# Three instead of four VectorE operations per Newton round of the layer norms of a two-layer decoder

## The reference

```
def _layernorm(x, axis=-1, eps=1e-05):
    m = jnp.mean(x, axis=axis, keepdims=True)
    v = jnp.var(x, axis=axis, keepdims=True)
    return (x - m) / jnp.sqrt(v + eps)

x = _layernorm(x + _L0_attn_ref(x, ...), axis=-1)     # norm 1
x = _layernorm(x + _L0_xattn_ref(x, ctx, ...), axis=-1)   # norm 2
x = _layernorm(x + _L0_ffn_ref(x, ...), axis=-1)      # norm 3
x = _layernorm(x + _L1_attn_ref(x, ...), axis=-1)     # norm 4
x = _layernorm(x + _L1_xattn_ref(x, ctx, ...), axis=-1)   # norm 5
x = _layernorm(x + _L1_ffn_ref(x, ...), axis=-1)      # norm 6
```

## Time and profile before

| | us |
|---|---|
| median of 3 runs | 2399.1 |
| lowest and highest | 2398.3 and 2404.93 |
| the profiled execution | 2404.64 |
| its span, first to last instruction | 2402.8 |

### The profile page before, as it was taken

The page is one execution under the profiler, slowest core; times in us unless marked ns, Lnnn a source line. Parts: engine busy times, 40 slices in busy tenths (PEclk is TensorE's granted clock), DMA queues, the critical chain, the costliest instruction groups (busy, mean ns, idle before and its releaser), DMA issues.

```text
span 2402.8 us, 41468 instructions
## 1 busy us (share of the span) xinstructions
PE 2027.9 (84%) x14592; PEld 1537.6 (64%) x14592; DVE 1495.6 (62%) x4040; ACT 821.1 (34%) x1665; POOL 910.0 (38%) x940
## 2 busy tenths in 40 slices
PE   5687889878998789887899878998789977899797
PEld 3444677655776467673776646865477655777586
DVE  5466466665775657756667657665576655765654
ACT  2112333342333334333343333333333342333342
POOL 2002533442335333353334433344233542335364
PEclk8577899998999789997899879999789988999898
DMA  5001000010000100001000000000000010000000
GB/s 155 3 1 31 3 1 1 1 32 3 3 1 2 34 3 1 1 2 34 3 1 2 21 15 3 2 1 23 13 3 1 1 33 1 3 1 1 11 1 5
DMA packets 25889, 27.75 MB, mean 12 GB/s; under 512 B 16482, under 2 KB 22348, under 8 KB 25188
## 3 DMA queue, kind: packets, MB, share of 16 engines
q1 hardware_dynamic: 25668, 24.88, 3.8%
HBM read 18.83 MB, written 1.05 MB: 8 GB/s over the span
## 4 chain that ended last, share of the span: by engine, by line
PE 53%; DVE 22%; issue 15%; POOL 7%; ACT 2%; DVEq 0%; POOLq 0%; ACTq 0%
PE ps L810 5%; PE ps L839 4%; PE ps L841 4%; PE ps L840 4%; DVE xmax_x L1547 4%; PE ps L858 4%; PE ps L859 4%; POOL xp_l L1210 3%; PE ps L860 3%; POOL pr_l L1210 3%; PE ps L976 3%; PE ps L872 2%; PE ps L963 2%; PE ps L964 2%; PE ps L855 2%
## 5 line engine op out<-in xcount | busy, mean ns | idle before, releaser
L1210 POOL TENSOR_TENSOR xp_l<-xp 128x512 f16<-128x512 f32 (+1 forms) x672 | 659.1, 982 | 1108.1 <-ACT xp L1119 1102.7
L1547 DVE TENSOR_REDUCE xmax_x<-ps 128x1 f32<-128x400 f32 (+1 forms) x768 | 430.0, 571 | 337.4 <-PE ps L810 320.8
L1119 ACT ACTIVATE xp<-ps 128x512 f32<-128x512 f32 (+1 forms) x672 | 381.1, 567 | 694.0 <-PE ps L841 691.1
L810 PE MATMUL ps<-cx_hl,xq_h 99*128 99x400 f16 (+1 forms) x768 | 280.1, 370 | 100.1 <-DVE xmax_x L1547 66.4
L858 PE MATMUL ps<-xp,cx_tok 128*97 128x256 bf16 (+1 forms) x1248 | 353.8, 284 | 5.3 <-ACT xo_x L1125 4.9
L841 PE MATMUL ps<-xq_h,cx_hl 96*128 96x256 f16 (+1 forms) x1248 | 354.9, 284 | 0.0
L839 PE MATMUL ps<-xq_h,cx_hl 99*128 99x256 f16 (+1 forms) x1248 | 353.9, 284 | 0.0
L840 PE MATMUL ps<-xq_l,cx_hl 99*128 99x256 f16 (+1 forms) x1248 | 352.2, 282 | 0.0
L859 PE MATMUL ps<-xp,cx_tok 128*97 128x256 bf16 (+1 forms) x1248 | 350.5, 281 | 0.0
L860 PE MATMUL ps<-xp_l,cx_tok 128*97 128x256 f16 (+1 forms) x1248 | 345.5, 277 | 0.0
L1210 POOL TENSOR_TENSOR pr_l<-pr 128x512 f16<-128x512 f32 x192 | 196.7, 1048 | 287.7 <-ACT pr L1091 287.3
(11 more groups left out here) (289 smaller groups left out, 3370.4 us busy)
## 6 DMA issues: line engine op xcount, KB each, us to landing
ct<-in_ctxT SPq DMA_DIRECT2D x8, 600.4 KB
c_tok<-in_ctx SPq DMA_DIRECT2D x8, 576.0 KB
cx_hl<-c_h SPq DMA_DIRECT2D x8, 309.6 KB
cx_hl<-c_l SPq DMA_DIRECT2D x8, 300.2 KB
c_wg<-in_wg SPq DMA_DIRECT2D x1, 1088.0 KB, 7.8
c_wu<-in_wu SPq DMA_DIRECT2D x1, 1088.0 KB, 9.8
c_wd<-in_wd SPq DMA_DIRECT2D x1, 1088.0 KB, 4.9
xin<-in_x SPq DMA_DIRECT2D x8, 128.0 KB, 2.1
```

What stands on the lines that cost most here:

```text
L810: mm(bank(bk, P, 0, n), qh[:, h, t * P:(t + 1) * P], c.h[:, k0:k0 + n], start=True, stop=True).then_inc(xa_x[i].sem, 1)
L1119: fn(xp_slot(i, n)[0:k_, 0:w], bank(b_s + n % 2, k_, 0, w), ACT.Exp, scale=scale).then_inc(xa_e[i].sem, 1)
L1210: sub = lambda out, a, b_: nc.gpsimd.tensor_tensor(out, a, b_, ALU.subtract)
L1547: red(side.xmax[:, t, c:c + 1], bank(bk, P, 0, CHUNKS[c][1]), AX.X, ALU.max).then_inc(xa_xd[i].sem, 1)
```

## The change

Each Newton round computes y <- y (1.5 - 0.5 var y y). Before: q = y y; q = q var; q = -0.5 q + 1.5; y = y q. After, the factor -0.5 goes into the first product and the sum with 1.5 into the last, each as a scalar_tensor_tensor, which does two operations on two tensors and a constant in one instruction. Three rounds in each of 48 norms have one instruction and one counted step fewer.

```
-STEPS = (126, 137, 182, 56, 45)
+STEPS = (114, 125, 164, 50, 39)
...
                 for _ in range(3):
-                    step(tt(q, y, y, ALU.mult))
+                    step(stt(q, y, -0.5, y, ALU.mult, ALU.mult))
                     settle()
                     step(tt(q, q, var, ALU.mult))
                     settle()
-                    step(ts(q, q, -0.5, 1.5, ALU.mult, ALU.add))
-                    settle()
-                    step(tt(y, y, q, ALU.mult))
+                    step(stt(y, q, 1.5, y, ALU.add, ALU.mult))
                     settle()
                     yield
```

## The result

The changed kernel takes 2410.07 us in the median of 6 runs (2408.38 to 2417.44), the kernel before 2402.24 us (6 runs, 2398.3 to 2406.17). The ratio is 1.0035 with a 95% interval of 1.0018 to 1.0052: 8 us slower, where 15.6 us faster was forecast. The profiled execution took 2417.44 us, its span is 2415.6 us, 12.8 more than the span before. It is the slowest of the six, so what is read from it adds up to 12.8 us and not to 8. One of the twelve runs of `only45` further down, 3291.83 us at a granted clock of 0.549, is left out of its ratio.

The account below looks back on a forecast made before the run. PE was taken to set the pace (84% busy), DVE mattering where PE waits behind it. Terms 3.1 + 1.8 + 3.0 + 3.0 + 4.7 = 15.6 us, off the median of 2399.1, gave 2383.5 us; range 2371 to 2394.

Parts of the forecast that it names:

- Norm 1: In each of six loop turns, PE waits for the xq_l pieces; 0.52 us saved per turn, 3.1 us.
- Norm 3: In the loop, PE's 0.67 us wait behind round one can vanish; 0.5 us per turn, 3.0 us.
- The ends: Outside the loop, PE waits for nine norms in the first batches and at the end; 0.52 us each, 4.7 us.
- norm 2: In the loop, PE's waits behind rounds one and three shorten; 0.3 us per turn on average, 1.8 us.
- Norm 6: In the loop, PE's waits behind rounds one and two shorten; 0.5 us per turn, 3.0 us.
- the rival of little gain: Fused forms cost 67 ns more, or PE's next waits fill those of norms 2, 3, 6; 2393.3 us, chance 0.15.
- the four terms: Loop savings at norms 1, 2, 3 and 6: 3.1, 1.8, 3.0 and 3.0 us.
- no wait is moved: Whole kernel: no DMA, wait or queue moves; only the chunk maxima, and PE through them, follow DVE earlier.
- a few us either way: TensorE's clock: the stretch behind norm 1's long wait stays; other stretches may move by a few us, inside the range.
- Norms 4 and 5: Hidden inside the loop by PE's gap at its end and DVE's 10.31 us idle; nothing gained there.
- The slower rival: At 24 places in the loop's norms, shifted rounds meet another 0.95 us POOL hold; 7.2 us slower, 2406, chance 0.04.

Follow-up runs that it names:

- only45: Kernel before with three operations per round in norms 4 and 5 alone, four in the others, near block uncut: 2410.5 us, ratio 1.0026.
- padded: Changed kernel's fused forms plus a neutral fourth counted operation (times one, plus zero) in each round: 2404.75 us, 0.9997 of the kernel before.
- again: The changed kernel run once more, nothing altered: 2411.43 us, 1.003 of the kernel before.
- split: Changed kernel, all norms at three operations, with VectorE's near-key block cut into four pieces: 2401.43 us, 0.9989 of the kernel before.
- split_b0n4: Changed kernel with the near-key block cut and four operations per round in norm 4 of batch 0 only: 2384.45 us, 0.9929 of the kernel before.
- delayed: Changed kernel, block uncut, with ten small neutral VectorE operations ahead of the negated maxima in the second self-attention: 2423.85 us, 1.0066 of the kernel before.
- split12346: Near-key block cut, three operations per round in all norms but norm 5: 2397.25 us, 0.9985 of the kernel before.
- split_five: Kernel before with a neutral fifth counted operation in each round and the near-key block cut: 2441.21 us, 1.0147 of the kernel before.
- before_split: Kernel before, four operations per round, with only the near-key block cut into four pieces: 2405.71 us, 1.001 of the kernel before.

## Why the prediction was wrong

**What held.** 144 instructions fewer; a free round of 0.59 us; no extra cost of the fused forms (`padded`); the busy time of the rounds, 35.3 us less. Norm 1: 6.6 us less wait against 3.1, 5.5 of them the wait for `xq_l`; but only 1.9 of these 5.5 in `again`, the same kernel. Norm 3: the 0.67 us gone and 0.25 more behind (0.25 to 0.50 at the next projection), 2.5 against 3.0. The ends: 0.61 against 0.52 at each of the two norms shown. That a hold passes to the next operation, as I had said of norm 1, is seen in the means of all the front norms' lines.

Norms 2 and 6 are the misses among the terms of the sum. At norm 2 the first wait lost 1.2 us over six turns, but the second stands in three turns more, 2.3 us: 1.1 us more wait, where 1.8 were to go. Norm 6 has 1.5 us more, where 3.0 were to go; its wait of 1.32 us became 1.54 and 0.35. Here the wait was filled by what PE waits for next, as the rival of little gain had it. The whole stretch from norm 2 to norm 6 did get shorter, by 5.3 us. In all, PE's waits at the four norms fell by 6.5 us in the changed kernel, by 3.0 in `again`, where the four terms sum to 10.9.

**The step that failed** is the sentence that no wait is moved and that PE follows the norms' earlier maxima, with the clock's other stretches set at "a few us either way". Sizes, from the starts of the norms' scaling operations, summed over the six turns:

| stretch | before | after | split | split_b0n4 |
|---|---|---|---|---|
| norm 4 to norm 1 | 382.0 | 385.6 | 388.0 | 384.0 |
| norm 1 to norm 2 | 271.4 | 269.6 | 275.8 | 269.1 |
| norm 2 to norm 6 | 105.1 | 99.8 | 97.3 | 100.3 |
| norm 6 to norm 3 | 538.1 | 540.0 | 540.7 | 538.0 |
| norm 3 to norm 4 | 431.6 | 445.6 | 424.5 | 425.4 |
| the loop | 1728.2 | 1740.6 | 1726.4 | 1716.8 |

The loop lost 12.4 us. The stretch from norm 3 to norm 4, where I had priced nothing, lost 14.0, 12.6 of them the new wait; the other stretches together gave back 1.6. Outside the loop, another 5.6 us, less 2.7 in the stretch behind, are batch 1's stretch at the lower clock. Without the two, the loop of `split_b0n4` is 11.4 us shorter than before, where the four terms of the forecast sum to 10.9, and the whole is 17 us faster by the ratio, where 15.6 was forecast. That agreement is luck: PE's waits at the four norms fell by 5.7 us only (63.3 to 57.6), its whole idle time in the loop by 5.6, and the other 5.8 us are PE busy for less time with the same matmuls (1479.6 instead of 1485.4 us). `split_b0n4` runs at a higher mean clock (0.903 against 0.897), so a part of the 17 us is clock and not steps.

**Norms 4 and 5.** "Hidden" was right of the work and wrong of the time: with all other norms at three operations, norm 4 of batch 0 decides whether a stretch that begins 100 us later runs at full clock. It is no rule for norm 4: changed with norm 5 alone (`only45`), it leaves that stretch as before, 86.6 us at 0.96. I costed a covered edit at nothing without asking what it shifts.

**The slower rival** had the mechanism, POOL holding one operation after another, but put it in the norms; it stood in another block, five holds in a row. That its price, 7.2 us, is near the 8 measured is luck: it came from 24 holds of 0.95 us in the norms, the loss from a wait of 2.10 us per turn and from the clock ahead of the loop. I had weighed holds only around the lines that the change touches. The Trainium skill, "SBUF — State Buffer", "Who interferes with whom", says that issue order decides who blocks, not the operation. The block agrees: in the kernel before, the pair of copies that starts at 1598.59, ahead of POOL's `pr_l` at 1598.81, takes 0.29 us, and the same pair behind it, at 1598.99, 1.13 us.

**Open.** Why the clock falls behind one 2.36-us wait and not behind the same wait in the next kernel was not settled. Its length, and PE's waits in the 28 us ahead of it, are the same to 0.01 us in the fourth turns of the kernels before and after, so it is not these alone. A longer wait (4.53 us) brought the fall in six turns of six.

## What to carry to other kernels

Where POOL and DVE hold each other, look for the longest run of DVE operations that POOL can hold, here ones with two SBUF inputs and copies, that stands close behind a stretch at the lower clock: here it was free only as long as the clock stayed down, and edits 100 us upstream ended that; cut such a block so that what PE waits for goes between its parts. When an edit that must be right gives nothing, compare the kernels stretch by stretch, work, waits and granted clock apart, before doubting its price. And test an edit place by place: here the best kernel leaves one of 48 norms as it was, and that was found by trial.

## What was not expected of the hardware

- A higher clock made a stretch slower: with the clock up behind the wait for `nms` the near block took 6.44 us and PE waited 2.10 us; with the clock down 2.65 to 4.85 us (in one turn of 37 5.78) and no such wait.
- Ahead of the loop the clock's fall goes with the kernel: in the five profiles with three operations in all of norms 1 to 4 of batch 0 and 1 (after, again, split, delayed, split12346) the stretch of batch 1 took 92.0 to 92.3 us, in the six with full clock there and norm 3 changed 84.8 us each. In the loop it also differs between executions: the same kernel had the clock up at the near block in six turns (after) and in four (again).
- Steps are not worth the same in both directions: with the block cut, a fifth step per round costs some 33 us by the ratios (`split_five` 1.0147 against `before_split` 1.001), taking the fourth away everywhere gives some 5 (`split` 0.9989), everywhere but in norm 4 of batch 0 some 19 (`split_b0n4` 0.9929).
